# A macaron block on one core: the second FFN's input transposed by VectorE and a DMA hop instead of TensorE

## What is computed

```python
x = x + 0.5 * ffn(_layernorm(x))      # "first FFN"
x = x + attn(_layernorm(x))           # 16 query heads, 4 key/value heads of 128, RoPE, window of 64 keys
x = x + 0.5 * ffn(_layernorm(x))      # "second FFN", the same weights

def ffn(x):
    w_q = clip(round(weight / (mean(abs(weight)) + 1e-5)), -1, 1)        # 256 x 256, ternary
    return einsum('bsi,oi->bso', layernorm(x) * ln_gamma + ln_beta, w_q) + bias
```

## Time and profile before

| | |
|---|---|
| median of 3 runs | 791.79 us (791.75 to 793.09) |
| profiled execution: its time, its span | 793.39 us, 790.5 us |
| TensorE busy | 778.3 us, 98% |
| VectorE, ScalarE, GpSimd busy | 626.1, 469.6, 455.7 us |
| DMA | 74.10 MB |
| chain that ended last | TensorE 92% |

### The profile page before, as it was taken

One profiled execution on the slowest core, in us unless ns is written; L12 is line 12 of the kernel. 1 busy time (PEld: TensorE's weight loads), 2 busy tenths in 40 slices (PEclk: granted clock), 3 DMA queues, 4 the chain that ended last, 5 costly groups with the idle time before them and its releaser, 6 DMA issues.

```text
span 790.5 us, 16087 instructions
## 1 busy us (share of the span) xinstructions
PE 778.3 (98%) x5630; PEld 727.2 (92%) x5630; DVE 626.1 (79%) x1321; ACT 469.6 (59%) x1602; POOL 455.7 (58%) x466
## 2 busy tenths in 40 slices
PE   8999999999999999999999999999999999999997
PEld 7688999999999999999999999999999999999996
DVE  5888967988688877888769887688867988688757
ACT  5366665657646565655747556475664657645574
POOL 3778555766446754567536773476635676446443
PEclk9999999999999999999999999999999999999999
DMA  8572324352252423425153242533224452243410
GB/s 300 114 194 59 90 55 120 95 127 48 55 152 63 121 54 89 126 55 120 41 135 94 68 99 49 134 92 97 67 55 121 94 129 45 57 104 68 107 29 27
DMA packets 54352, 74.10 MB, mean 94 GB/s; under 512 B 7168, under 2 KB 30208, under 8 KB 54272
## 3 DMA queue, kind: packets, MB, share of 16 engines
q1 hardware_dynamic: 53712, 72.74, 37.7%
q10 hardware_dynamic: 560, 0.34, 0.2%
HBM read 14.33 MB, written 4.19 MB: 23 GB/s over the span
## 4 chain that ended last, share of the span: by engine, by line
PE 92%; DVE 3%; POOL 2%; DMA 1%; issue 1%; ACT 0%; SPq 0%; DVEq 0%; POOLq 0%
PE job_p L656 33%; PE attn_p L656 22%; PE scores_p L673 13%; PE heads_p L656 11%; PE probsT_p L737 7%; PE job_p L833 4%; PE job_p L817 2%; POOL q_s L1282 1%; DMA x_res<-wo 1%; POOL probs L1271 1%; DMA x_in<-x 0%; DVE parts L1015 0%; DMA rope_swap<-rope_sin 0%; POOL wo_s L1253 0%; DVE rope_sin L934 0%
## 5 line engine op out<-in xcount | busy, mean ns | idle before, releaser
L656 PE MATMUL attn_p<-wo_s,headsT 128*128 128x256 f32 x1536 | 209.2, 286 | 1.0 <-ACT headsT L1175 0.7
L656 PE MATMUL job_p<-xnT,wq_s 128*128 128x512 f32 x768 | 205.3, 403 | 1.2 <-DVE v_s L951 1.1
L656 PEld LDWEIGHTS attn_p<-wo_s,headsT 128*128 128x128 f32 x1536 | 196.5, 191 | 7.0 <-ACT headsT L1175 1.4
L1154 ACT ACTIVATE probs<-scores_p,neg_max 128x96 f32<-128x96 f32 x512 | 167.6, 352 | 51.8 <-DVE neg_max L900 51.6
L1271 POOL TENSOR_TENSOR probs<-probs,inv_sum 128x384 f32<-128x384 f32 x128 | 107.9, 843 | 152.0 <-DVE inv_sum L906 151.9
L1282 POOL TENSOR_TENSOR q_s<-q_s,rope_swap 128x512 f32<-128x512 f32 x128 | 164.3, 1291 | 52.3 <-DMA rope_swap<-rope_sin 52.2
L1175 ACT ACTIVATE headsT<-heads_p,columns_s 128x512 fp32r<-128x512 f32 x128 | 88.0, 688 | 140.9 <-PE heads_p L656 140.5
L656 PEld LDWEIGHTS job_p<-xnT,wq_s 128*128 128x128 f32 x768 | 135.8, 189 | 26.6 <-DVE v_s L951 1.7
L934 DVE SCALAR_TENSOR_TENSOR rope_sin<-job_p,columns_s,rope_t 128x512 f32<-128x512 f32 x160 | 118.9, 743 | 21.1 <-PE job_p L656 19.9
L673 PE MATMUL scores_p<-k_s,q_s 128*128 128x96 f32 (+2 forms) x1024 | 131.6, 272 | 0.3 <-POOL q_s L1282 0.2
L673 PEld LDWEIGHTS scores_p<-k_s,q_s 128*128 128x128 f32 x1024 | 126.5, 192 | 3.4 <-POOL q_s L1282 1.1
(11 more groups left out here) (96 smaller groups left out, 972.7 us busy)
## 6 DMA issues: line engine op xcount, KB each, us to landing
rope_swap<-rope_sin SPq DMA_DIRECT2D x320, 128.0 KB, 2.3
v_odd<-v_s SPq DMA_DIRECT2D x64, 192.0 KB, 3.3
x_in<-x SPq DMA_DIRECT2D x15, 256.0 KB, 4.2
out<-x_res SPq DMA_DIRECT2D x15, 256.0 KB, 2.5
x_tr<-x_transposed SPq DMA_DIRECT2D x7, 512.0 KB, 5.3
q_s<-wq SPq DMA_DIRECT2D x3, 512.0 KB, 10.1
q_s<-wo SPq DMA_DIRECT2D x2, 512.0 KB, 10.6
x_res<-wo SPq DMA_DIRECT2D x2, 512.0 KB, 4.8
```

The lines of the kernel that those rows point to most:

```text
L656: mm = nc.tensor.matmul(dst, a(p), b(q), start=clears and i == 0, stop=len(pairs) == 1, skip_group_check=True)
L1154: ins = nc.scalar.activation(probs[:, i, k, 0:REACH], scores_p[i][:, k, 0:REACH], ACT.Exp, bias=neg_max[:, i, k:k + 1], accum_out=row_sum[ ...
```

## The change

The 14 jobs YT2 leave TensorE. For batches 0 to 6 the two normalised halves are written into `y` in an order of 32-column blocks (`y_block`, `source_block`), VectorE transposes the whole buffer of 128x1024 in place, in blocks of 32x32 (`turn`), SyncE sends it to a DRAM buffer `hop` of 128x1024 (`send`, one DMA of 512 KB), and brings it back with four DMAs of 128 KB that put each block on its partitions (`land`, into `x_tr`). ScalarE and VectorE then make `lnT` from `x_tr`, as they do for the first FFN; the low part takes four instructions of 128x128 for a half instead of two of 128x256 (`ln_pieces`).

`x_tr` now has one more user. So `loadt`, which stood near the start of a middle batch, waits for the low part of YT1p and stands behind `land`. The middle and last orders of all five tables are new. The first batch, the prologue and what follows the last batch's T14 are the same.

The table TENSOR, the start of its middle order:

```diff
-        K1c Q4c S0c Q5c O13p W14p T15p S1c V10c O14p W15p Q6c T0c Q7c
-        O15p S2c YT0p W0c K2c T1c S3c Q8c YT1p O0c W1c T2c S4c Q9c
-        O1c W2c T3c FO0p S5c V11c Q10c O2c FO1p W3c T4c S6c Q11c O3c
+        K1c O13p W14p T15p Q4c S0c Q5c S1c O14p V10c W15p Q6c T0c O15p
+        Q7c S2c W0c T1c K2c S3c Q8c O0c W1c Q9c T2c V11c S4c O1c
+        W2c T3c S5c Q10c O2c W3c T4c S6c Q11c FO0p O3c W4c T5c S7c
+        K3c FO1p O4c W5c T6c Q12c O5c Q13c S8c W6c FO0n T7c S9c Q14c
```

The table SYNC, its middle order:

```diff
-        K1c loadt0n Q4c Q5c Q6c load0n Q7c K2c Q8c Q9c Q10c store0p Q11c store1p
-        K3c shift1c Q12c Q13c Q14c Q15c K0n Q0n Q1n Q2n Q3n shift0n
+        K1c Q4c load0n Q5c Q6c Q7c K2c Q8c send0p land0p shift1c Q9c Q10c loadt0n
+        Q11c store0p store1p K3c Q12c Q13c Q14c Q15c K0n Q0n Q1n Q2n Q3n shift0n
```

In the middle order of SCALAR, up to heads5c:

```diff
+        probsT14p heads14p exp0c probsT15p exp1c V10c heads15p mask2c mask3c probsT0c probsT1c exp2c norm0p heads0c
+        norm1p exp3c heads1c mask4c mask5c probsT2c V11c heads2c probsT3c exp4c exp5c mask6c heads3c YT0p
+        probsT4c mask7c YT1p heads4c probsT5c exp6c YT0n YT1n mask8c heads5c exp7c probsT6c mask9c exp8c
```

The code:

```diff
+    hop = {"YT2": nc.dram_tensor("hop", (P, BLOCKS * E), F32).ap()}
...
+        y_flat = y[:, :, :, :].rearrange("p m k e -> p (m k e)")
+        y_turn = y_flat.rearrange("p (j c m k b) -> p j c m k b", j=4, c=EC, m=2, k=2)
+        x_flat = x_tr[:, :, :].rearrange("p c n -> p (c n)")
+        x_turn = x_flat.rearrange("p (i c m k b) -> p i c m k b", i=4, c=EC, m=2, k=2)
...
+            def send(x):
+                sp.wait_ge(y_turned, TURNS[x[0].replace("send", "turn"), *x[1:]] + 1)
+                sp.dma_start(hop[turned_name(x)[0]], y_flat).then_inc(y_sent, 16)
+
+            def land(x):
...
+                sp.wait_ge(y_sent, 16 * (SENDS[x[0].replace("land", "send"), *x[1:]] + 1))
...
+                    sp.wait_ge(centered, CENTERED["center", 1, b + 1] + 1)
+                for i in range(4):
+                    sp.dma_start(x_flat[:, i * E:(i + 1) * E],
+                                 hop[kind][32 * i:32 * (i + 1), :].rearrange("a (j f) -> j a f", j=4)).then_inc(landed, 16)
...
             def load_transposed(x):
                 sp.wait_ge(ffn_added, FFN_OUT["FO1", 1, b - 1] + 1)
+                if b > 1:
+                    sp.wait_ge(ln_lo, FFN_IN["YT2", 1, b - 2] + 1)
...
+            def turn(x):
+                first = Y_HALVES[turned_name(x)]
+                for n in (first, first + 1):
+                    wait_y(dve, n)
+                nc.vector.transpose(y_flat, y_flat).then_inc(y_turned, 1)
...
             def ffn_in_high(x):
+                if turned(x):
+                    wait_landed(act, x)
+                    act.wait_ge(job_ready, JOBS[list(FFN_OUT)[n - 2]] + 1)
```

More of the change, by code:

```diff
@@ L110 @@
     "middle": """
[L111 to L115, removed]
@@ L119 @@
+        max6c YT0p probsT4c heads3c YT1p Q11c FO0p heads4c probsT5c inv6c max7c FO1p K3c YT0n
+        heads5c Q12c inv7c YT1n probsT6c max8c Q13c max9c heads6c inv8c FO0n Q14c probsT7c FO1n
+        astats0n astats1n heads7c inv9c probsT8c Q15c max10c heads8c XT0n XT1n max11c inv10c probsT9c K0n
+        inv11c heads9c probsT10c max12c Q0n inv12c heads10c max13c probsT11c Q1n V00n heads11c probsT12c inv13c
+        max14c Q2n inv14c max15c heads12c Q3n probsT13c inv15c V01n
     """,
     "last": """
-        heads13p K1c probsT14p evac0p stats0p Q4c max0c heads14p probsT15p max1c inv0c Q5c inv1c V10c
@@ L122 @@
[L122 to L126, removed]
@@ L127 @@
-        evac0c stats0c inv14c heads12c max15c probsT13c norm0c inv15c heads13c probsT14c evac1c stats2c heads14c probsT15c
-        norm2c YT0c YT2c heads15c FO0c evac2c stats3c tailb3c YT3c FO2c tailc3c FO3c
+        probsT14p heads13p K1c Q4c max0c probsT15p evac0p heads14p max1c stats0p Q5c inv0c inv1c heads15p
+        V10c Q6c max2c probsT0c Q7c evac1p stats1p heads0c max3c K2c inv2c turn0p probsT1c Q8c
+        heads1c inv3c max4c Q9c probsT2c Q10c max5c probsT3c inv4c heads2c Q11c YT0p V11c probsT4c
@@ L147 @@
     "middle": """
-        probsT14p heads14p probsT15p exp0c exp1c V10c heads15p probsT0c mask2c norm0p mask3c YT0p exp2c heads0c
-        norm1p probsT1c mask4c exp3c mask5c heads1c probsT2c YT1p exp4c heads2c YT0n V11c probsT3c exp5c
-        mask6c probsT4c heads3c mask7c exp6c probsT5c heads4c mask8c exp7c heads5c probsT6c YT1n mask9c heads6c
-        probsT7c exp8c exp9c heads7c mask10c mask11c probsT8c anorm0n anorm1n XT0n heads8c XT1n exp10c probsT9c
-        exp11c mask12c mask13c probsT10c heads9c exp12c V00n mask14c heads10c probsT11c exp13c mask15c probsT12c heads11c
@@ L154 @@
+        probsT9c exp11c mask13c heads9c probsT10c exp12c mask14c heads10c probsT11c exp13c V00n mask15c probsT12c heads11c
+        exp14c mask0n probsT13c heads12c exp15c mask1n V01n heads13c
     """,
     "last": """
-        probsT14p heads14p probsT15p exp0c exp1c mask2c V10c heads15p probsT0c norm0p mask3c exp2c heads0c YT0p
-        mask4c probsT1c exp3c mask5c norm1p probsT2c heads1c YT1p heads2c probsT3c exp4c V11c mask6c exp5c
-        mask7c probsT4c heads3c exp6c heads4c mask8c probsT5c heads5c probsT6c exp7c exp8c mask9c mask10c heads6c
@@ L159 @@
[L159 to L160 removed]
+        probsT14p heads14p probsT15p exp0c exp1c mask2c heads15p V10c probsT0c exp2c mask3c heads0c norm0p norm1p
+        exp3c mask4c mask5c probsT1c heads1c probsT2c exp4c heads2c probsT3c YT0p mask6c exp5c V11c probsT4c
+        heads3c YT1p heads4c exp6c mask7c probsT5c mask8c heads5c exp7c mask9c probsT6c exp8c mask10c heads6c
@@ L528, in transposed_part @@
             width = block_count(x) * P
+            if turned(x):
+                return x_turn[:, :, e, x[1], :, :]
             if from_x(x):
```

167 lines of the change are left out of this document (117 added, 50 removed).

## The result

The changed kernel takes **794.69 us** (median of 20 runs, 792.13 to 797.57) against 792.41 us for the kernel before (20 runs, 789.81 to 794.33). The ratio is 1.0027, with a 95% interval of 1.0016 to 1.0039: slower by 0.3%, where 0.5% faster was forecast. The profiled execution spans 791.5 us (its own time is 793.26), that of before 790.5.

The account below looks back on a forecast made before the run. TensorE was taken to bound the kernel; 790.5 - 6.0 given back + 2.0 of waits = 786.5, with 2.9 around it 789.4, for the median 791.79 - 4.0 = 787.8 us, range 785.6 to 789.9.

Parts of the forecast that it names:

- chain 1: Exchange of y through DRAM up to FO0p: landing at 34.3 us after K1c, 2.7 us of slack.
- limit of 37.0: Latest landing, in us after K1c, said to cost FO0p nothing.
- rival 2: loadt later than forecast, holding up O5c: 1.0 to 1.4 us lost a batch; 793 us, 790 to 796; 12%.
- rival 3: VectorE too full, slow transpose and low parts: waits of 0.5 to 1 us a batch; 790 us, 788 to 795; 10%.
- Rival 1: Landing on four of 16 DMA engines takes 8.7 us, 2.5 us late at FO0p: 805 us, 790 to 805; 22%.
- turns the sign: Landing transfer time, 7.0 us, at which a slow landing turns the forecast gain into a measurable loss.
- Chain 2: loadt, issued after YT1p, lands at median 46.9, needed by 46.6 for O5c: 2 us in six batches, bounds 0 and 8.
- What TensorE gives back: Transposes off TensorE, with changed neighbours: 0.86 us a batch, 6.0 us over seven, bounds 5.0 and 6.1.
- rival 4: Nothing to see: what the removed transposes give back goes into neighbours' waits, time stays at 791.8 us; 5%.
- VectorE's sum: Added transposes and low parts: 1.8 us a batch, 13 us in seven, VectorE busy 639 of 785 us, 81%.

Follow-up runs that it names:

- e1_k16: Changed kernel with its four landing DMAs cut so that they spread over 16 engines: 788.53 us, ratio to before 0.9942.
- e7_k16_short_turn: e1_k16 with VectorE's transpose cut to 32 of 1024 columns (second FFN's input wrong): 788.84 us, ratio to before 0.9958.
- e6_shift_back: Changed kernel, landing still on four engines, with shift1c moved behind K3c in SyncE's middle order: 819.75 us, ratio to before 1.0345.

## Why the prediction was wrong, point by point

**What fell** is one step of chain 1: "the last lands some 3.3 us after its issue, as the 192 KB pieces of `v_odd` do", which put the landing at 34.3. The rows that I took as like it are transfers over 64 or 128 partitions on both sides. Measured, ScalarE began at 36.8 to 38.8 us after K1c instead of finding its operand at 34.3, against a limit of 37.0. In e1_k16, where only the cut of the transfer differs, the last landing is at 32.9 to 33.8. The time alone would not tell this: 794.7 also lies in the ranges that rival 2 (790 to 796) and rival 3 (788 to 795) had. The wait in front of FO0p, e1_k16 and e7_k16_short_turn do.

**Rival 1** had the mechanism: four of sixteen engines. The Trainium skill (DMA: Bandwidth & Descriptors, "Why a DMA increments its semaphore by 16 and not by 1") states it as a rule; the shares of the two coarse cuts agree (0.24 to 0.27 for four engines, 0.13 to 0.14 for two), and with a cut that allows sixteen the share rises to 0.76. I gave it 22% and should have given it more than the forecast, since no row spoke against it, only the absence of such a transfer in the kernel before. Its size was off: 8.7 us for the bytes at 15 GB/s an engine, the mean over the run; an engine of the four moves about 23 GB/s, so they take 6. Around the bytes it had 1.5 us in all; measured are 1.5 ahead of them and some 1.6 behind. ScalarE started in time in two of the six middle batches and up to 1.8 us late in the others, instead of 2.5 late in all, and the time 794.7 instead of 805. The price at which it "turns the sign", 7.0 us of transfer and 1.5 around it, 8.5 together, came close: 8.4 to 9.6 us passed from the first issue to ScalarE's start.

**Chain 1, the rest** held: `turn` ends at 25.80 (predicted 25.7), `send` has landed at 28.5 to 29.2 (29.2), FO0p stands at 38.75 when nothing is late (38.6), VectorE's transpose takes 1.23 us (1.19).

**Chain 2** cost next to nothing (2 us predicted, bounds 0 and 8). (The forecast's own range ended at 789.9, though its bounds, 5.0 us given back and 8 lost here, add up to 794.8.) `loadt` landed after 3.8 to 5.8 us, and VectorE was through with YT1p as reckoned. In e1_k16 it is issued 41.5 us after K1c in every batch.

**What TensorE gives back.** I had 6.0 us over seven batches. e1_k16, where nothing waits for the exchange, shows 2.2 in the six middle batches (568.93 to 566.73) and 1.7 in the last (96.00 to 94.31): 3.9. By the job prices of the rows the new order does take 0.87 us less a batch, but 0.4 to 0.7 of it goes back into small waits that the windows count as busy: 0.11 us before W1c, 0.21 before W8c, in some batches 0.1 to 0.2 before Q13c. This is what rival 4 described, at half its size. TensorE of e1_k16 around W8c shows how such a wait looks:

```profile
373.47 1.88 PE L764 MATMUL attn_p<-wo_s,headsT 128*128 128x256 f32 x12
375.19 0.89 PE L764 MATMUL heads_p<-probsT,v_s 128*128 128x256 f32 x6
```

From O7c to W8c pass 1.72 us. Behind a scores job an O takes 1.51 or 1.52, like the one at 335.17 behind a narrow job in the earlier trace rows; its last six matmuls wanted the low part of heads7c.

**VectorE's sum** was right, 638.6 us for 639, in part by luck. The two terms that it had came as foreseen: the transposes 8.6 us (8.4), the low parts of the exchange 3.8 more than before (4.2). Two that it had not nearly cancel: the pieces of `loadt` take 7.1 us more, and the small instructions of the statistics, which meet GpSimd less often in the new order, 5.1 less. Rival 3 (VectorE too full) is refuted by e7.

**The ledger** of the profiled spans, after less before: +2.05 us in the six middle batches, +0.08 in the last, -1.1 in the first batch and the tail, together +1.0. With the landing cut anew the same sum is -5.0: -2.2, -1.7, and -1.1. The -1.1 is no gain of the change: it lies ahead of batch 1, where no order changed, and that stretch varies from 120.8 to 125.1 us over the profiled executions of the kernels here. Without it the ledger has +2.1 us, and the medians say +2.3; with the new cut it has -3.9, and they say -4.3. So the landing on four engines cost 6.0 us, more than the 3.9 that the change brings without it.

## What to carry to other kernels

A new transfer is priced by its shape before its size. Look at the slowest dimension of both sides: a source that began with 4 kept the DMA share at 0.27 and took 6 us for 524 KB, one that began with 2 kept it at 0.13, and 32 on both sides took 3 us. Then look at the DMA share while it runs: here a steady 0.25 with a reader waiting was a quarter of the engines, and the cut could be changed without touching anything else. And when an operand moves from PSUM to SBUF, or a queue is rearranged, look at what GpSimd does at that moment: in e6_shift_back TensorE waited about 3 us in most batches, and the run took 25 us longer, though TensorE's own work had not changed.
